# The layer's one-hot by destination: four compares on GpSimd between the gathers, in place of one on VectorE

## What is computed

```python
edge_features = jnp.concatenate([x[row], x[col], radial], axis=-1)   # row: source, col: destination
h = silu(edge_features @ Wm1 + bm1)
h = silu(h @ Wm2 + bm2)
messages = h @ Wm3 + bm3
out = jax.ops.segment_sum(messages, col, num_segments=x.shape[0])
u = silu(jnp.concatenate([x, out], axis=-1) @ Wu1 + bu1)
u = silu((u @ Wu2 + bu2) @ Wi1 + bi1) @ Wi2 + bi2
x = layernorm(x + u)
```

## Time and profile before

| | us |
|---|---|
| timed runs, median (lowest to highest) | 2136.04 (2135.17 to 2136.64) |
| profiled execution, span | 2718.3 |
| GpSimd: first gather starts | 47.19 |
| GpSimd: gathers end, scatters begin | 1265.48 |
| GpSimd: last scatter starts | 2593.01 |
| gathers, 784: busy, mean | 748.5, 0.955 |
| scatters, 784: busy, mean | 755.2, 0.963 |

### The profile page before, as it was taken

One profiled execution on the slowest core, in us unless ns is written; L12 is line 12 of the kernel. 1 busy time (PEld: TensorE's weight loads), 2 busy tenths in 40 slices (PEclk: granted clock), 3 DMA queues, 4 the chain that ended last, 5 costly groups with the idle time before them and its releaser, 6 DMA issues.

```text
span 2718.3 us, 44066 instructions
## 1 busy us (share of the span) xinstructions
PE 1765.2 (65%) x12349; PEld 1539.3 (57%) x12447; DVE 1663.9 (61%) x5512; ACT 1366.4 (50%) x3959; POOL 1503.9 (55%) x1572
## 2 busy tenths in 40 slices
PE   5487778788887887776733333676665565576670
PEld 5366666666666676665633323666654554565660
DVE  4565667666666666786534534777755455465668
ACT  3466666666666666885424433666543232232224
POOL 2466666666666666655556665565555545545510
PEclk9698889989889999988755556777777777777795
DMA  6365655554333333333523434666555554456541
GB/s 189 87 146 125 148 125 143 132 134 120 86 83 88 84 86 86 84 80 104 130 81 99 100 98 127 186 171 175 169 153 153 147 158 138 139 164 173 161 134 48
DMA packets 336885, 342.10 MB, mean 126 GB/s; under 512 B 67138, under 2 KB 266684, under 8 KB 336634
## 3 DMA queue, kind: packets, MB, share of 16 engines
q1 hardware_dynamic: 279998, 231.80, 33.2%
q0 software_dynamic: 50176, 104.07, 12.7%
q10 hardware_dynamic: 6460, 3.34, 0.5%
HBM read 246.09 MB, written 90.16 MB: 124 GB/s over the span
## 4 chain that ended last, share of the span: by engine, by line
PE 33%; issue 20%; DVE 16%; another core or an unknown queue 13%; ACT 10%; DVEq 2%; SPq 2%; DMA 0%; ACTq 0%
PE bank L1633 8%; PE bank L998 5%; PE bank L1286 4%; PE bank L1612 4%; PE bank L1298 3%; PE bank L1295 3%; PE bank L1259 3%; DVEq L739 2%; ACT L760 2%; ACT L1078 2%; DVE rt L975 1%; ACT ring L1064 1%; ACT ra L1069 1%; DVE ring L966 1%
## 5 line engine op out<-in xcount | busy, mean ns | idle before, releaser
L921 POOL DMA_INDIRECT gtab<-ring,idx x784 | 755.2, 963 | 573.6 <-ACT ring L940 256.1
L1048 POOL DMA_INDIRECT ra<-ptab,gis x784 | 748.5, 955 | 516.2 <-remote 211.0
L998 PE MATMUL bank<-ring 128*128 128x78 f32 x1568 | 307.5, 350 | 277.0 <-issue 242.3
L937 ACT ACTIVATE rt<-rt 128x256 f32<-128x256 f32 x536 | 216.7, 406 | 501.6 <-DVE rt L977 344.4
L998 PEld LDWEIGHTS bank<-ring 128*128 128x128 f32 x1568 | 281.8, 262 | 292.1 <-issue 254.3
L1298 PEld LDWEIGHTS bank<-cst,ra 128*128 128x128 f32 x1568 | 224.9, 200 | 184.5 <-issue 184.0
L1064 ACT ACTIVATE ring<-bank 128x512 f32<-128x512 f32 x196 | 116.6, 595 | 365.4 <-remote 348.4
L1286 PE MATMUL bank<-wm,ring 128*128 128x128 f32 x1568 | 249.8, 302 | 55.9 <-issue 47.7
L1298 PE MATMUL bank<-cst,ra 128*128 128x128 f32 x1568 | 238.1, 285 | 63.8 <-issue 63.0
L1633 PE MATMUL bank<-ring 128*128 128x130 f32 x1312 | 222.1, 322 | 80.1 <-issue 60.4
L1286 PEld LDWEIGHTS bank<-wm,ring 128*128 128x128 f32 x1568 | 237.8, 214 | 61.2 <-issue 49.4
(11 more groups left out here) (284 smaller groups left out, 3669.9 us busy)
## 6 DMA issues: line engine op xcount, KB each, us to landing
ring<-in_edge_attr SPq DMA_DIRECT2D x196, 256.0 KB
ring<-gtab SPq DMA_DIRECT2D x89, 393.0 KB
gtab<-ring SPq DMA_DIRECT2D x36, 687.8 KB
ra<-in_edge_weight SPq DMA_DIRECT2D x132, 128.0 KB
ring<-gtab SPq DMA_DIRECT2D x49, 327.5 KB
ring<-reld SPq DMA_DIRECT2D x196, 78.0 KB
ring<-gtab SPq DMA_DIRECT2D x49, 262.0 KB
ra<-ptab,gis POOLq DMA_INDIRECT x784
```

The lines of the kernel that those rows point to most:

```text
L921: G.indirect_dma_start(out=gtab[group_of(i)][:, :], out_offset=bass.IndirectOffsetOnAxis(ap=idx[:, n, i:i + 1], axis=0), in_=row[i % NE][: ...
L937: k = S.activation(prl[i % NPR][:, n, :], prl[i % NPR][:, n, :], ACT.Identity, accum_out=lgs[i % 2][:, n:n + 1])
L998: k = T.matmul(bk[:, 256:256 + W], row[i % NE][:, n, 0:H], od2[i % NO2][:, n, :], start=(first and n == 0), stop=(n == 3), skip_group_chec ...
L1048: G.indirect_dma_start(out=gp[i % NGP][:, n, :], out_offset=None, in_=ptab[:, :], in_offset=bass.IndirectOffsetOnAxis(ap=gis[:, n, i:i + 1 ...
```

## The change

The compare leaves VectorE's loop. GpSimd builds the same tile with four instructions, one per slot, 128 x 78 each, against the column numbers in `iota` (in SBUF; VectorE used a copy in PSUM). They stand between the second and the third gather of a tick, for the chunk that is six ticks behind (VectorE did it five behind). GpSimd waits for the offsets (`rel`), the constants (`cst`) and the buffer (`w`); the fourth compare releases `od`.

```diff
             for t in TICKS:
                 i = chunk(t, 0)
+
+                def gather(n):
+                    G.indirect_dma_start(
+                        out=gp[i % NGP][:, n, :], out_offset=None, in_=ptab[:, :],
+                        in_offset=bass.IndirectOffsetOnAxis(ap=gis[:, n, i:i + 1], axis=0)).then_inc(s[f"gp{i % NGP}"], 16)
+
                 if i is not None:
                     e.wait_ge(s["h1p"], i + 1 - NGP)
+                    gather(0)
+                    gather(1)
+                j = chunk(t, 6)
+                if j is not None:
+                    e.wait_ge(s["rel"], 2)
+                    e.wait_ge(s["cst"], 16)
+                    e.wait_ge(s["w"], j - NOD + 1)
                     for n in range(4):
-                        G.indirect_dma_start(
-                            out=gp[i % NGP][:, n, :], out_offset=None, in_=ptab[:, :],
-                            in_offset=bass.IndirectOffsetOnAxis(ap=gis[:, n, i:i + 1], axis=0)).then_inc(s[f"gp{i % NGP}"], 16)
+                        k = G.tensor_scalar(ohd[j % NOD][:, n, :], iota[:, 0:W], rel[:, n, j:j + 1], None, ALU.is_equal)
+                    k.then_inc(s["od"], 1)
+                if i is not None:
+                    gather(2)
+                    gather(3)
             for i in range(RE):
                 rows_pool(e, i)
...
-                i = chunk(t, 5)
-                if i is not None:
-                    e.wait_ge(s["w"], i - NOD + 1)
-                    V.tensor_tensor(ohd[i % NOD], iotap[:, 0:W].rearrange("p (o b) -> p o b", o=1).to_broadcast([P, 4, W]),
-                                    rel[:, :, i:i + 1].to_broadcast([P, 4, W]), ALU.is_equal).then_inc(s["od"], 1)
```

## The result

The changed kernel takes 2532.3 us (median, 2529.6 to 2535.29) against 2136.34 us for the kernel before, with a fourth run beside its three (2135.17 to 2139.71): 396 us slower, a ratio of 1.184 (95% interval 1.183 to 1.186). The forecast was 2319 us with a range of 2130 to 2480. The direction was right; the loss is more than twice the forecast, and outside the range.

What follows compares the result with a forecast made beforehand. The prediction took GpSimd's in-order queue to bound the layer and the scatters in timed runs. 2136 us plus 186 for the compares, less 8 of slack, plus 5 at the seam, gave 2319 us, range 2130 to 2480.

Steps and rivals of the forecast that it cites:

- The floor of 2169 us: GpSimd's queue, whole kernel: 99.3 us to the first release, gathers 953.0, scatters 992.5, tail 124.3.
- the 549 us of waits: GpSimd's waits in the profiled execution, 213 us in the layer and 336 among the scatters, claimed nearly all gone when timed.
- The scaling by 2136/2718: Shrinks the 193 us outside GpSimd's stream (start, first wait, tail) to 152, making the floor 2128 us.
- the slack of 8 us: GpSimd's remaining waits in a timed run, floor of 2128 us against the median; subtracted from the forecast.
- the port: GpSimd's compares may be held up by VectorE's through a shared port: at most 0.48 us per tick, 94 us.
- The term of 186 us: Cost of the added GpSimd compares: 4 x 0.237 = 0.95 us a chunk, over 196 chunks.
- The double row: Upper end for GpSimd's compares: 4 x 0.47 = 1.9 us a chunk, 372 us, giving 2508 us.
- (c): Rival: every return from compares to gathers costs GpSimd 0.88 us, 172 us on top, 2491 us; chance 0.10.
- The seam: Between last gather and first scatter, GpSimd makes six steps of compares alone and waits: 0 to 8 us, taken as 5.
- VectorE's relief: Removing VectorE's compare frees 0.39 us a chunk, 76 us of VectorE, but shortens nothing.
- (a): Rival: the compares hide in GpSimd's 1.12 us of wait per layer tick, time stays 2136 us; chance 0.10.
- (b): Rival: the VectorE and TensorE chain sets the layer's tick, so VectorE's 0.39 us come back, 2060 us; chance 0.14.

Runs made afterwards that it cites:

- no_vector_compare_c: The kernel before with VectorE's compare left out from the second use of each buffer on; 2138.0 us, ratio 1.001.
- after: The changed kernel itself, four GpSimd compares a chunk in place of VectorE's one; 2532.3 us against 2136.34 for the kernel before, ratio 1.184.
- compares_first: The changed kernel with its four compares ahead of a chunk's first gather; 2890.3 us, ratio 1.060 to the kernel before on the same chip.

## Why the prediction was wrong, point by point

**The bound: right, for a wrong reason.** "In a timed run GpSimd's queue is the bound" is shown by no_vector_compare_c. The floor of 2169 us by adding up GpSimd's own steps was good reasoning: its two main terms, 953.0 and 992.5, are there again in no_vector_compare_c: 958.6 us from the 25th gather (81.60) to the first scatter (1040.15), 990.2 from there to the last. But the 549 us of waits were not a stretching by the profiler. They belong to the second level of the kernel, which timed runs on two chips show as well. Profiled executions at level 2136 agree with their timed runs (2138.2 for 2140.07). The scaling by 2136/2718, and the slack of 8 us that came out of it, have no basis. The 33 us by which the timed runs lay under the floor are in two other terms, which the second level had made longer: the 25th gather starts at 81.60 in place of 99.30, and the tail after the last scatter's end is 107.0 in place of 124.3. That the scaled 152 us come near the true ones (157), and the 8 us near the 7.4 of waits in the layer, is luck.

**The compare's price: the step that failed.** I took VectorE's row of a 128x78 addition, 0.237 us, with the words "nearer to the second row, and I know of no reason that GpSimd does it faster". That reason speaks only against less, not against more. It is 0.50 us (0.465 with VectorE idle, 1.86/4; the rest goes with VectorE's work beside it, see the port below). The term of 186 us should have been 390. The double row, 4 x 0.47 = 1.9 us and 2508 us in the end, stood in the text as the upper bound of the cost and was then left outside the range; it was the nearest of all. Where no row shows an operation on that engine, the row of another engine is no middle value: here it was less than half of the price, and the range has to hold the pessimistic one. (The range was said to take in nearly all of (c), but (c)'s own value, 2491, lies above its end of 2480.) The fixed part alone, 0.29 us, is above the value that I took for the whole, and it is paid four times a chunk, since GpSimd got four instructions where VectorE had one. The memsets of 0.10 us overlap (0.03 us apart), and said nothing of it.

The Trainium skill's factor (GPSIMD Engine Reference, section 3: VectorE about twice as fast) was used to confirm 0.95 us a chunk. That section's figure is measured on one wide addition, N = 2048. Here four compares take 2.02 us against 0.475 for VectorE's one of the same 128x312 elements, a factor of 4.25: the factor of two doesn't hold for one wide instruction cut into four short ones. By the prices above one GpSimd instruction of 312 columns would take 0.29 + 311 x 0.0028 = 1.16 us, an estimate, 2.4 times VectorE's. No run has it, and it is the obvious version left untried.

**The port: a part of the loss, inside its bounds.** In a tick where VectorE's 78x512 compare L1228 runs beside, the four last 2.23 us (802.62), in one where nothing of VectorE runs, 1.86 (809.85). Counted over the 185 groups of four between 100 and 1410 us that the timeline shows unmixed: 1.86 in all 7 beside which VectorE does nothing, 1.88 in the mean of 67 beside other instructions of VectorE, 2.12 in the mean of 111 beside L1228. So nearly all of the lengthening goes with this one instruction, and not with VectorE's being busy. The mean of the groups is 2.02, so (2.02 - 1.86) x 196 = 31 us of the loss go with VectorE's work beside it; I had 0 in the forecast and up to 94 in the range. L1228 lasts 0.57 us in the mean against 0.50 in no_vector_compare_c, which costs nothing as VectorE isn't the bound. The group in the tick shown, by the length of one compare (shortest, median, longest, in ns):

```profile
L1061 POOL TENSOR_SCALAR ring<-cst,rel x4: 468/494/846, 802.6 to 804.4; 128x78 f32<-128x78 f32 x4
```

One compare of the four takes nearly the whole delay. And in the 43 groups where L1228 starts 0.23 to 0.49 us after the first compare, it ends 1.04 to 1.07 us after it, wherever it started, as if it were held until one point of the group. The Trainium skill's exclusive lock (SBUF — State Buffer, "SBUF: two separate sides") lets whichever of the two starts first have the port for its whole instruction, while the other blocks. These rows look like such a lock and not like a sharing in proportion; the delays, 0.4 us of the group and up to 0.36 of L1228, stay under a whole instruction's length. That it is the port is argued from the rows, no run separates it. The gathers feel less of it: in the kernel before those beside L1218 last 0.98 us in the mean (161 of them), the others 0.95, so the one row was not the whole of it.

**The seam: right in kind.** In the timeline of GpSimd after the last gather:

```profile
1416.02 0.94 POOL L1047 DMA_INDIRECT ra<-ptab,gis  x1 [0.30 <-issue]
1417.00 9.48 POOL L1061 TENSOR_SCALAR ring<-cst,rel 128x78 f32<-128x78 f32 x20
1429.52 1.84 POOL L1061 TENSOR_SCALAR ring<-cst,rel 128x78 f32<-128x78 f32 x4 [3.04 <-PE bank L1269]
1431.52 1.06 POOL L921 DMA_INDIRECT gtab<-ring,idx  x1 [0.16 <-issue]
```

Six steps of compares alone, 24 of the 784, and one wait of 3.04 us for the scatter matmul, where I took 5 in all. After it the scatters run at 1.27 us a step: 991.8 us for 783 steps.

**VectorE's relief at nothing, the other waits at nothing: right.** Without VectorE's compare the ratio was 0.999, 0.999 and 1.001 on three chips. The wait for `w` shows up nowhere but at the seam.

**The sum as it should have been,** from no_vector_compare_c (span 2138.2, last gather at 1038.90) to after (2528.8, 1416.02): 377.1 in the layer up to the last gather, 14.3 at the seam (15.50 in place of 1.25 us from last gather to first scatter; 11.3 of it are the last 24 compares), the scatters +1.7, the tail -2.4: 390.7, to rounding the difference of the spans.

**The rivals.** (a) is true at level 2700 only. (b)'s mechanism exists, but with GpSimd out of the way by a gather, not as the kernel stands. (c), a fixed cost of returning from compares to gathers, is there with 0.10 us a chunk instead of 0.88: 20 us, and the shorter gaps around the compares give about as much back.

**The profiled execution.** I expected a span of 2700 to 2800 us. It was taken at level 2136 and measured 2528.8. At level 2700 the sister kernel compares_first had 2891.

**What stays open.** What makes the second level. At it GpSimd, TensorE and ScalarE have idle time that the trace puts down to "issue" or "remote", in the layer about 1 us a tick and among the scatters some 340 us in all, and the granted clock is lower (0.787 over the span of the earlier trace rows against 0.870 in no_vector_compare_c); which of these is cause and which effect, no run shows. In the layer nearly all of it is there with four gathers only: the last gather comes at 1264 and 1270 us against 1039 at level 2136, with three gathers at 1044 and 1049 against 1009. The changed kernel itself wasn't run there. No version tried that keeps the whole computation beats the kernel before.

## What to carry to other kernels

An engine whose mean busy share is low can be the bound all the same: count its queue by start to start distances, fixed gaps included, and see whether the sum of its steps reaches the timed span. Don't put work into that queue; taking work off another engine gave nothing here until it was shortened. And see how far behind the next engine is before you count on shortening it: here it was 0.15 us a tick. Price an operation that moves to GpSimd by instruction count first (about 0.29 us each here before the first column), and when no row of the trace shows it, keep the pessimistic bound inside the range.

## What the runs showed of the hardware that I hadn't expected

- A GpSimd compare with a per-partition scalar: 0.29 us plus 2.8 ns a float32 column; 0.09 us less with a constant.
- The same program has two levels, 2136 and 2700 to 2740 us, by the chip (three of one sort, two of the other), the first repeatable to 0.3% between lowest and highest, the second to 1 and 2%. A profile and a median can come from different levels: where the span is far above the timed median, that is to be settled before its waits are read.
- TensorE's clock after a wait. In the changed kernel's tick the eight matmuls of L1269 last 1.97 us, twice the 1.01 of the earlier trace rows, after 3.11 us of waiting. The granted clock (the third number from the right) of that stretch and of the end of the tick:

```profile
805.10:807.10 2.00, 1.99 (x13) 2.00 (x14) 0.00 (x0) 0.00 (x0) 1.70 (x2) 0.50 0.34 89
...
811.00:812.00 1.00, 1.00 (x10) 1.00 (x9) 0.00 (x0) 0.99 (x3) 0.83 (x3) 0.88 0.00 0
```

The clock is at its lower level, 1.2 GHz, when the work comes back, and it returns within the tick. Here it costs nothing, as TensorE waits for GpSimd again. It does mean that the busy time of an engine that waits more looks bigger (TensorE 956 us in the layer against 837 in no_vector_compare_c) with no work added.
